# RWKV layer of a six-layer kernel: the product of exp(k) and v moved from VectorE to GpSimd, by way of a copy of v made on ScalarE

## The reference, cut to what matters

```python
x = x + _L0_attn_ref(_layernorm(x), ...)

# inside:
x = _layernorm(x, ln_g, ln_b)
last_x = jnp.pad(x[:, :-1], ((0, 0), (1, 0), (0, 0)))
k = (x * time_mix_k + last_x * (1.0 - time_mix_k)) @ Wk.T
v = (x * time_mix_v + last_x * (1.0 - time_mix_v)) @ Wv.T
r = (x * time_mix_r + last_x * (1.0 - time_mix_r)) @ Wr.T
td = jnp.exp(time_decay)
# for every token t, with exp(k) as k:
#   den = den * td + k[t];  num = num * td + k[t] * v[t];  wkv[t] = num / (den + 1e-08)
out = jax.nn.sigmoid(r) * wkv @ Wo.T
```

## Time and profile before

| what | us |
|---|---|
| median of three runs | 1769.66 |
| the profiled execution, device time | 1754.2 |
| its span, first to last instruction | 1752.5 |
| VectorE busy over the span | 1345.0 (77%) |
| GpSimd busy over the span | 1075.9 (61%) |
| ScalarE busy over the span | 1023.6 (58%) |
| first and last product L1790 of the RWKV layer start at | 347.8 and 501.4 |

### The profile page before, as it was taken

The page is one execution under the profiler, slowest core; times in us unless marked ns, Lnnn a source line. Parts: engine busy times, 40 slices in busy tenths (PEclk is TensorE's granted clock), DMA queues, the critical chain, the costliest instruction groups (busy, mean ns, idle before and its releaser), DMA issues.

```text
span 1752.5 us, 39134 instructions
## 1 busy us (share of the span) xinstructions
PE 1474.8 (84%) x10452; PEld 1356.7 (77%) x10452; DVE 1345.0 (77%) x3991; ACT 1023.6 (58%) x2541; POOL 1075.9 (61%) x1700
## 2 busy tenths in 40 slices
PE   8799999788857999998529999586999985089996
PEld 8699999667746999998319999585888874089996
DVE  7789998799988888887737777574877857267775
ACT  4588888433316888884126666334777721056764
POOL 7438887777743354533774666531898856746665
PEclk9999999899978999997669999756998965589998
DMA  6110110930001111100312221212222201122210
GB/s 193 49 38 32 37 30 13 211 86 1 0 1 56 38 32 37 32 7 7 149 54 61 64 64 50 76 32 76 85 85 73 74 1 46 53 64 64 65 51 11
DMA packets 93268, 96.23 MB, mean 55 GB/s; under 512 B 12072, under 2 KB 75709, under 8 KB 92576
## 3 DMA queue, kind: packets, MB, share of 16 engines
q1 hardware_dynamic: 83168, 76.70, 15.3%
q0 software_dynamic: 9920, 17.35, 3.0%
HBM read 63.75 MB, written 33.78 MB: 56 GB/s over the span
## 4 chain that ended last, share of the span: by engine, by line
PE 60%; DVE 12%; POOL 12%; issue 11%; ACT 3%; DMA 1%; DVEq 0%; SPq 0%; POOLq 0%; ACTq 0%
PE banks L586 5%; POOL rt_rows L840 5%; PE banks L575 4%; PE banks L1188 3%; PE banks L566 3%; PE banks L1175 3%; PE banks L567 3%; PE banks L568 3%; PE banks L1177 3%; PE banks L1176 3%; PE banks L1190 3%; PE banks L1189 3%; PE banks L1210 3%; PE banks L587 2%; PE banks L1160 2%
## 5 line engine op out<-in xcount | busy, mean ns | idle before, releaser
L1433 DVE TENSOR_TENSOR choice_hlo<-choice_h,choice_hhi 128x512 fp32r<-128x512 f32 x256 | 177.3, 733 | 21.3 <-ACT choice_hhi L1286 20.3
L1278 ACT ACTIVATE choice_h<-banks 128x512 f32<-128x512 f32 x256 | 152.5, 600 | 58.6 <-PE banks L1177 47.8
L799 DVE SCALAR_TENSOR_TENSOR top_h<-top_silu,top_xs,banks 128x176 f32<-128x176 f32 x364 | 128.5, 394 | 56.2 <-ACT top_silu L644 56.2
L840 POOL DMA_INDIRECT rt_rows<-X,top_slot x128 | 128.4, 1003 | 44.9 <-issue 37.6
L644 ACT ACTIVATE top_silu<-banks,top_xs 128x352 f32<-128x352 f32 x182 | 101.1, 555 | 87.8 <-PE banks L568 87.8
L1175 PE MATMUL banks<-choice_xin_hi,ec_w_hi 128*128 128x256 f32 x512 | 145.0, 283 | 4.8 <-ACT choice_xin_lo L1271 3.6
L1188 PE MATMUL banks<-choice_hhi,ec_w_hi 128*128 128x256 f32 x512 | 145.9, 285 | 3.2 <-DVE choice_hlo L1433 2.5
L1286 ACT ACTIVATE choice_hhi<-choice_h 128x512 fp32r<-128x512 f32 x256 | 146.6, 625 | 0.0
L1527 POOL TENSOR_SCALAR choice_y_hi_lo<-choice_yw 128x512 fp32r<-128x512 f32 x64 | 42.3, 661 | 166.2 <-ACT choice_yw L1301 165.2
L1176 PE MATMUL banks<-choice_xin_lo,ec_w_hi 128*128 128x256 f32 x512 | 143.1, 280 | 0.0
L1177 PE MATMUL banks<-choice_xin_hi,ec_w_lo 128*128 128x256 f32 x512 | 143.0, 279 | 0.0
(11 more groups left out here) (310 smaller groups left out, 5394.5 us busy)
## 6 DMA issues: line engine op xcount, KB each, us to landing
choice_token_row<-choice_tokens SPq DMA_DIRECT2D x64, 256.0 KB, 3.1
mlstm_run_row<-mlstm_run SPq DMA_DIRECT2D x32, 512.0 KB, 3.6
rt_rows<-rt_blank SPq DMA_DIRECT2D x2, 6188.0 KB, 37.9
top_xs<-rt_rows SPq DMA_DIRECT2D x182, 68.0 KB, 1.9
X<-in_x SPq DMA_DIRECT2D x8, 512.0 KB, 6.9
ec_stage<-in_ec_w SPq DMA_DIRECT2D x2, 2048.0 KB, 12.5
X<-rt_y SPq DMA_DIRECT2D x8, 512.0 KB, 6.9
rt_rows<-X,top_slot POOLq DMA_INDIRECT x128, 2.3
```

Source lines behind the costliest of these rows:

```text
L840: pool.indirect_dma_start(d.region[self.run], bass.IndirectOffsetOnAxis(ap=self.slot[:, t:t + 1], axis=0), self.sh.rows[:, t, :], None).th ...
L1433: dve.tensor_tensor(flat(self.hlo), self.h[:, c, :], flat(self.hhi).bitcast(F32), ALU.subtract).then_inc(self.hlo_done, 1)
```

## The change

- ScalarE: behind exp(k) of a batch it copies v from PSUM into a new tile `v`. Both operations count up `ek_done`, so that its count is 2b+1 behind exp(k) of batch b and 2b+2 behind the copy. Before exp(k) it now also waits that the product of batch b-2 is done.
- VectorE: the product is gone. It starts with the scan of den once exp(k) is there, and waits for the product before the scan of num.
- GpSimd: the new function `ekv` multiplies `v` and `ek`. It stands between `norm` of batch s+2 and `er1` of batch s, and waits for the scans of batch b-2 and for the copy of v. In step 1 the order is ekv(0), er1(0), ekv(1), er1(1).
- The new tile is 2 x 256 float32 per partition, behind the layer's other tiles.

```diff
         def exps(b, u):
             act.wait_ge(self.kv_done, b + 1)
             need(act, self.scans_done, b - 1)
+            need(act, self.ekv_done, b - 1)
             act.activation(self.ek[:, u, :], self.pkv[u][:, 0:T], ACT.Exp).then_inc(self.ek_done, 1)
+            act.activation(self.v[:, u, :], self.pkv[u][:, T:2 * T], ACT.Copy).then_inc(self.ek_done, 1)
             act.wait_ge(self.r_done, b + 1)
...
         def mix(b, u):
             last = lambda part: part(dve, self.layer + 1, b - 1, 1 - u)
             td = self.td[:, 0:1].to_broadcast([P, T])
-            dve.wait_ge(self.ek_done, b + 1)
-            dve.tensor_tensor(self.ekv[:, u, :], self.pkv[u][:, T:2 * T], self.ek[:, u, :], ALU.mult).then_inc(self.ekv_done, 1)
+            dve.wait_ge(self.ek_done, 2 * b + 1)
             dve.tensor_tensor_scan(self.den[:, u, :], td, self.ek[:, u, :], 0.0, ALU.mult, ALU.add)
             dve.wait_ge(self.ekv_done, b + 1)
...
+        def ekv(b, u):
+            apart(pool, self.scans_done, b - 1, self.sh.passed)
+            apart(pool, self.ek_done, 2 * b + 2, self.sh.passed)
+            pool.tensor_tensor(self.ekv[:, u, :], self.v[:, u, :], self.ek[:, u, :], ALU.mult).then_inc(self.ekv_done, 1)
...
         def step(s, u):
             if isinstance(s, int) and s == 1:
-                er1(0, 0)
-                er1(1, 1)
+                for b in range(2):
+                    ekv(b, b)
+                    er1(b, b)
                 norm(3, 1)
                 self.sh.moments.scale(pool, self.layer, B - 1, 1)
                 return
             if inside(s + 2):
                 norm(s + 2, u)
             if inside(s):
+                ekv(s, u)
                 er1(s, u)
             self.scale_next(pool, s - 2, u)
```

More of the change, by code:

```diff
@@ L1635, in __init__ @@
         self.x1 = f("x1", [P, 2, T + 1])
-        self.ek, self.er, self.er1, self.ekv, self.num, self.den, self.under, self.over, self.z = (
-            f(n, [P, 2, T]) for n in ("ek", "er", "er1", "ekv", "num", "den", "under", "over", "z"))
+        self.ek, self.er, self.er1, self.ekv, self.num, self.den, self.under, self.over, self.z, self.v = (
+            f(n, [P, 2, T]) for n in ("ek", "er", "er1", "ekv", "num", "den", "under", "over", "z", "v"))
         bk = sh.banks
```

## The result

The changed kernel takes 1776.74 us (median of 20 runs, 1768.61 to 1786.46) where the kernel before takes 1772.11 (20 runs, 1762.35 to 1782.47). The ratio is 1.0037 with a 95% interval of 1.0021 to 1.0053: 6.6 us slower, 3.7 to 9.4 (the two medians alone differ by 4.6), under the 1% that counts as a change here. The forecast was 5.8 us slower, 1775.5. A second set of runs, 12 against 23 on another chip, gave 1.0034 (1.001 to 1.0059).

A forecast was written before the change was run, and what follows sets the result against it. VectorE was taken to bound the layer. Waiting for GpSimd, +0.17 x 31 = +5.3 us, plus 0.5 at the start gave +5.8 on the median of 1769.66, rounded to 1775.5 us; range 1763 to 1784.

The forecast's parts named there:

- VectorE bounds the layer and 0.33 a batch is on its path: RWKV layer: VectorE sets the 4.96 us pace; removing its product frees 0.33 a batch, 10.2 us at most.
- Copy on ScalarE at nothing: ScalarE behind exp(k): the 0.38 us copy of v ends before exp(-r) can start, so it costs nothing.
- GpSimd's product at 0.72: GpSimd: the product of two full 256-element inputs takes 0.72 us, from a line through 128 and 512 elements.
- VectorE's instructions with two SBUF inputs and GpSimd's exclude each other: den, num, under and z take turns with GpSimd's SBUF reads; VectorE lets go about 0.2 early, GpSimd 0.12.
- rival 3: Turns between VectorE and GpSimd: exclusion to each instruction's very end, +0.46 a batch, 1784.5 us; chance 0.08.
- The exchange, pace 5.13: Steady batch: GpSimd's product falls between z and den, num starts 1.64 behind z; +0.17 a batch, +5.3 us.
- rival 2: Turn behind z: product comes too late, den goes first, num near 1.81; +0.37 a batch, 1781.7 us; chance 0.13.
- other way round: Turn at z: product asks just before z, z held to some 0.5, num near 1.7; +0.24 instead of +0.17.
- Rival 1: Den scan doesn't wait for GpSimd's product; a two-batch loop binds at 4.79 a batch, 1764.9 us; chance 0.17.
- Rival 4: GpSimd becomes the bound: product costs 1.09, num 0.37 later still, +0.54 a batch, 1786.9 us; chance 0.08.
- Start 0.5: Layer's start: GpSimd is free for the first product only at 348.85, under moves later; +0.3 to +0.7, taken as 0.5.
- Sum: Whole kernel: +5.3 us over the batches plus 0.5 at the layer's start, +5.8 us in all.

The follow-up runs named there:

- a: Kernel before with the product exp(k) * v left out, the num scan running over exp(k): pace 4.63 us a batch, ratio 0.9949 to the kernel before.
- b: Kernel before plus ScalarE's copy of v, unused; VectorE's product only waits for it: pace 4.95 us, one run, 1752.95 us against 1751.32.
- d: Changed kernel with the decay of both scans read from PSUM instead of SBUF: pace 4.74 us, ratio 0.9949 to the kernel before.
- e: Kernel before with the decay of both scans read from PSUM, product still on VectorE: pace 4.83 us, ratio 0.9968 to the kernel before.
- k: Changed kernel with the reciprocal written to PSUM, so z has one SBUF input: pace 5.00 us, ratio 1.0008 to the kernel before.
- c: Kernel before plus the copy of v and a GpSimd product into a tile nobody reads: pace 5.16 us, ratio 1.0056 to the kernel before.
- j: Changed kernel with the decay in PSUM and 1 + exp(-r) made on ScalarE: pace 4.74 us, ratio 0.9962 to the kernel before.
- f: Changed kernel with the copy of v put behind exp(-r) on ScalarE: pace 5.37 us, ratio 1.0087 to the kernel before.

## Why the prediction was right, point by point

- **VectorE bounds the layer and 0.33 a batch is on its path.** Right: a gives 0.33.
- **Copy on ScalarE at nothing.** Right, as b's trace shows it. It starts 0.28 behind exp(k), not 0.38, so v comes a tenth earlier than reckoned.
- **GpSimd's product at 0.72.** Right: 720 ns at least, 1.7 times VectorE's 0.42. By the Trainium skill's factor of about two (GPSIMD Engine Reference, Engine selection) it would have been 0.84, an estimate; the trace does not bear that out at this size.
- **VectorE's instructions with two SBUF inputs and GpSimd's exclude each other.** Right, and now shown: d, e and k each move one operand into PSUM and the stretching of that instruction is gone. The Trainium skill (SBUF — State Buffer, Who interferes with whom) states this exclusion, and also that an instruction of VectorE with at most one SBUF input, outside its 2-port perf modes, does not contend with GpSimd. It has the lock held for the whole instruction; in c den starts behind GpSimd's product as if this were let go 426.11 + 0.84 - (426.62 + 0.88 - 0.68) = 0.13 before its end, where the prediction had 0.12. The strict form of rival 3 is wrong in size.
- **The exchange, pace 5.13.** The mechanism is right; the term was too small: 5.20. c runs at 5.13 throughout and the changed kernel for three batches, so the arithmetic of this order holds. (As an increase it was put too low: num moves from 1.44 to 1.64 behind z, which is +0.20 on the batch of 4.93 that the working uses; the +0.17 comes from setting 5.13 against the mean of 4.96. c's steady part gives +0.18.) But it is mostly not the order that the changed kernel is in. The prediction noted against rival 2 that a late product undoes itself in the next batch, and stopped there; it had to ask whether the one after is late again. It is: 5.35 and 5.00 average 5.18, +0.22 in place of +0.17. The "other way round" had been put at num 1.7 behind z and is 1.51. The order of the turns in it was right; but it had the product ask just before z, so that z starts 0.5 late. The product asks 0.22 ahead, and z is 0.36 late.
- **Rival 1** (a loop over two batches at 4.79) is where d and j run, at 4.74, in batches of 4.57 and 4.92: once the turns are out, this is the next bound. **Rival 4** has a slip that nothing rests on: at its pace of 5.50, GpSimd's round of 5.32 ends ahead of the next z and adds nothing.
- **Start 0.5.** 0.4.
- **Sum.** 7.9 us in the trace, 6.6 in the runs, 5.8 forecast. 1.1 of the trace's 7.9 is in one batch of 6.27 us, below. That the sum comes so near is partly luck: the changed kernel's batches lie on either side of the one that was reckoned with, and their mean happens to be close to it.

## What to carry to other kernels

Before work moves between VectorE and GpSimd, count the SBUF inputs of what runs beside it, not the busy shares: an instruction that reads PSUM on VectorE may be the only one that disturbs nobody, and moving it to GpSimd puts a longer one in line with every two-input neighbour. The cure can be one operand: with the scans' decay in PSUM the changed kernel goes from 1.0037 to 0.9949 of the kernel before. But hold every variant against the one that differs from it in that alone: the same cure takes the kernel before to 0.9968, and once it is in, no run shows that the moved product pays. And where a result depends on the batch two back, work out two batches in a row: a rule that corrects each batch by the one before can settle into two alternating paces, and the mean is then neither.

## What was not expected of the hardware

TensorE's granted clock is low in the first batches of the layer in both kernels (0.50 from 354 to 356 us). Between 360 and 500 us it stays at 1.00 in the kernel before; in the changed kernel it falls once more. Busy times of the changed kernel in stretches of 2 us (columns as above; PEclk is the granted clock as a share of 2.4 GHz):

```profile
446.00:448.00 2.00, 0.87 (x7) 0.68 (x7) 2.00 (x6) 0.40 (x2) 2.00 (x4) 1.00 0.00 0
448.00:450.00 2.00, 1.70 (x13) 1.50 (x12) 1.98 (x7) 0.95 (x2) 1.71 (x4) 0.89 0.00 0
450.00:452.00 2.00, 2.00 (x6) 1.65 (x5) 1.91 (x4) 0.00 (x0) 0.78 (x2) 0.50 0.00 0
452.00:454.00 2.00, 2.00 (x11) 1.68 (x11) 0.69 (x1) 1.04 (x3) 0.67 (x1) 0.75 0.00 0
```

The clock goes to 0.50, the 1.2 GHz level, for some 3 us, after a stretch in which TensorE was busy for 0.87 of 2 us while it waited for a held z. Over 365 to 485 us it was busy for 100.98 us, 104.44 before. At the low clock a pair of projection matmuls takes 1.06 in place of 0.59, and that batch 6.27 us in place of 5.2. The second trace of the changed kernel has the same, at another place (0.50 from 440 to 442 us, a batch of 6.64), and so has f (0.50 from 366 to 368 us, the batch of 7.19). None of the other traces has a low clock between 362 and 490 us.

What brings it on is not shown. The wait for a held z before this fall is 1.13 us, and it is 1.13 in the batch at 426 us too, where the clock stays at 1.00. So a loss on VectorE of 0.2 a batch can come with a small second one on TensorE, in these traces one batch in the layer.
